# Query halves of every other tile for layer 1's product with the values

## The reference

```python
def _L1_attn_ref(x, w_attn, w_proj):
    B, T, N_EMBD, N_HEAD = (4, 1024, 96, 6)
    qkv = x @ w_attn
    q, k, v = jnp.split(qkv, 3, axis=-1)
    ...
    att = jnp.einsum('bqhd,bkhd->bhqk', q, k) * scale
    causal = jnp.tril(jnp.ones((t, t), dtype=bool))
    att = jnp.where(causal[None, None], att, jnp.finfo(att.dtype).min)
    att = jax.nn.softmax(att, axis=-1)
    out = jnp.einsum('bhqk,bkhd->bqhd', att, v).reshape(b, t, c)
    return out @ w_proj
```

## Time and profile before

| | |
|---|---|
| median of 3 runs | 2108.75 us (2106.65 to 2112.81) |
| span of the profiled execution | 2107.2 us |
| TensorE busy | 1847.2 us (88%) |
| VectorE busy | 1248.2 us (59%) |
| ScalarE busy | 1119.8 us (53%) |
| GpSimd busy | 144.7 us (7%) |

### The profile page before, as it was taken

One profiled execution on the slowest core, in us unless ns is written; L12 is line 12 of the kernel. 1 busy time (PEld: TensorE's weight loads), 2 busy tenths in 40 slices (PEclk: granted clock), 3 DMA queues, 4 the chain that ended last, 5 costly groups with the idle time before them and its releaser, 6 DMA issues.

```text
span 2107.2 us, 25342 instructions
## 1 busy us (share of the span) xinstructions
PE 1847.2 (88%) x9408; PEld 742.6 (35%) x9408; DVE 1248.2 (59%) x2508; ACT 1119.8 (53%) x1423; POOL 144.7 (7%) x69
## 2 busy tenths in 40 slices
PE   2697589998899988998899988999889988999858
PEld 1132233343234433343333432344333433334323
DVE  5671676546764667636765467636676466744631
ACT  2256345674456744675456744567345745555433
POOL 3000002000020000200020000200002000200000
PEclk7599599999999999999999999999999999999979
DMA  6416400354016320263003440163202630002100
GB/s 139 58 35 110 75 12 19 86 66 83 11 30 116 68 39 18 51 101 68 21 19 86 66 83 11 30 116 70 37 19 51 101 68 15 17 11 59 27 11 8
DMA packets 55699, 110.98 MB, mean 53 GB/s; under 512 B 17686, under 2 KB 18903, under 8 KB 54040
## 3 DMA queue, kind: packets, MB, share of 16 engines
q1 hardware_dynamic: 54040, 109.06, 27.5%
q10 hardware_dynamic: 1536, 0.30, 0.1%
HBM read 61.82 MB, written 34.60 MB: 46 GB/s over the span
## 4 chain that ended last, share of the span: by engine, by line
PE 68%; DVE 18%; ACT 5%; DMA 4%; issue 3%; SPq 1%; POOL 1%; ACTq 0%; DVEq 0%; POOLq 0%
PE psOM L645 16%; PE psS L591 12%; PE psT L620 8%; DVE mx L1279 8%; PE psT L621 7%; PE psT L755 6%; PE psS L769 4%; PE psT L623 4%; DVE mrow L1381 3%; PE psT L541 3%; DVE qb L1408 2%; DVE x L1390 1%; PE psT L550 1%; DMA qr<-negb 1%; PE psT L800 1%
## 5 line engine op out<-in xcount | busy, mean ns | idle before, releaser
L1006 ACT ACTIVATE probs<-psT 128x1024 f32<-128x1024 f32 (+7 forms) x768 | 622.7, 837 | 524.3 <-PE psT L621 258.2
L1279 DVE TENSOR_REDUCE mx<-psS 128x1 f32<-128x512 f32 (+3 forms) x1152 | 704.9, 643 | 286.2 <-PE psS L591 217.2
L621 PE MATMUL psT<-qb,kb 97*128 97x512 f32 x768 | 415.6, 585 | 0.0
L645 PE MATMUL psOM<-probs,v 128*32 128x512 f32 (+3 forms) x2688 | 383.3, 558 | 11.6 <-ACT probs L1006 11.6
L591 PE MATMUL psS<-ka,qa 128*128 128x512 bf16 x768 | 298.8, 400 | 38.9 <-DVE mx L1279 19.8
L620 PE MATMUL psT<-qa,ka 128*128 128x512 bf16 x768 | 296.8, 386 | 11.8 <-DVE resid L1268 5.1
L755 PE MATMUL psT<-xf,w1s 97*128 97x512 f32 x384 | 187.8, 623 | 2.1 <-DVE mrow L1381 1.8
L623 PE MATMUL psT<-qr,kr 97*128 97x512 bf16 (+3 forms) x576 | 184.2, 349 | 4.3 <-DMA qr<-negb 3.3
L1408 DVE TENSOR_TENSOR qb<-psOM,qa 32x768 fp32r<-32x768 f32 x128 | 121.8, 952 | 101.6 <-ACT qa L1046 99.7
L769 PE MATMUL psS<-probs,w2s 128*96 128x512 f32 x384 | 180.7, 596 | 0.8 <-ACT att L1071 0.8
L591 PEld LDWEIGHTS psS<-ka,qa 128*128 128x128 bf16 x768 | 71.5, 97 | 308.8 <-DVE mx L1279 244.3
(11 more groups left out here) (146 smaller groups left out, 1651.3 us busy)
## 6 DMA issues: line engine op xcount, KB each, us to landing
scr<-split SPq DMA_DIRECT2D x32, 576.0 KB, 4.4
scr<-qb SPq DMA_DIRECT2D x16, 768.0 KB, 6.8
qr<-scr SPq DMA_DIRECT2D x48, 192.0 KB, 6.5
au<-ot SPq DMA_DIRECT2D x192, 32.0 KB, 2.0
lb<-ot SPq DMA_DIRECT2D x192, 32.0 KB, 2.0
qr<-scr SPq DMA_DIRECT2D x48, 128.0 KB, 4.4
kr<-scr SPq DMA_DIRECT2D x48, 128.0 KB, 7.3
qa<-scr SPq DMA_DIRECT2D x32, 128.0 KB, 3.7
```

The lines of the kernel that those rows point to most:

```text
L621: last = mm(o[:, a:b], kb[:, h, ks], qb[:, h, a:b], start=False, stop=True)
L645: last = mm(psO[j:j + 2 * HD, a - c * HALF:HALF], v[:, kt, 2 * p + hh, :], probs[:, (2 * kt + hh) % 4, a:(c + 1) * HALF], start=kt == 0, s ...
L1006: A(probs[:, n % 4, q0:T], psT[:, t_slot(ts, m), q0:T], ACT.Exp).then_inc(t_free, 1)
L1279: V.reduce_max(mx[layer][:, p % 2, (h % 2) * NT + t, kc:kc + 1], psS[:, s_bank(st, fill), 0:max_cols(layer, t, kc)], AX).then_inc(s_free, 1)
```

## The change

In layer 1's value product, a query half c now is the query tiles c, c + 2, c + 4, c + 6, in place of the tiles 4 c to 4 c + 3. For key tile kt, half 0 has the even query tiles from kt on, and half 1 the odd ones. The tiles of a half stand side by side in psO as before, so the moving operand is read from probs as blocks of 128 columns that lie 256 apart. att then holds the tiles in that order, and `res_norm` finds tile t at column 128 x `tile_at(1, t)`. Layer 0's matmuls are those of before, in another branch of the code.

```diff
@@ -216,6 +216,11 @@
 def att_m(layer, p):
 
     return ("attn1", p - 1) if layer else ("attn0", p - 1) if p else ("lead", 0)
+
+
+def tile_at(layer, t):
+
+    return t % NC * (NT // NC) + t // NC if layer else t
 
 
 def next_layer0(it):
@@ -629,7 +634,6 @@
 
                 def values(p, kt):
 
-                    q0 = q_from(layer, kt)
                     if kt == 0:
                         if layer == 1 and p == 0:
                             pe.wait_ge(y_free, upto("y_free", it, st, 0))
@@ -638,12 +642,18 @@
                         ts, n = att_t(layer, (p * NT + kt) * 2 + hh)
                         pe.wait_ge(t_free, upto("t_free", it, ts, n + 1))
                         for c in range(NC):
-                            a, j = max(q0, c * HALF), 32 * (2 * hh + c)
-                            if a >= (c + 1) * HALF:
+                            j = 32 * (2 * hh + c)
+                            if layer == 0:
+                                last = mm(psO[j:j + 2 * HD, :], v[:, kt, 2 * p + hh, :],
+                                          probs[:, (2 * kt + hh) % 4, c * HALF:(c + 1) * HALF], start=kt == 0,
+                                          stop=kt == NT - 1)
                                 continue
-                            end = NT if layer == 0 else (c + 1) * HALF // P
-                            last = mm(psO[j:j + 2 * HD, a - c * HALF:HALF], v[:, kt, 2 * p + hh, :],
-                                      probs[:, (2 * kt + hh) % 4, a:(c + 1) * HALF], start=kt == 0, stop=kt == end - 1)
+                            first = (kt + NC - 1 - c) // NC
+                            if first == NT // NC:
+                                continue
+                            every = probs[:, (2 * kt + hh) % 4, :].rearrange("p (i c q) -> p c i q", c=NC, q=P)
+                            last = mm(psO[j:j + 2 * HD, first * P:HALF], v[:, kt, 2 * p + hh, :], every[:, c, first:],
+                                      start=kt == 0, stop=kt == NT - NC + c)
                         last.then_inc(p_used, 1)
 
                 n = PER_PAIR[layer]
@@ -705,8 +715,8 @@
                     pe.wait_ge(s_free, upto("s_free", it, "norm", b - 1))
                     for i in range(4):
                         t = 4 * b + i
-                        last = mm(psS[:, b, i * C:(i + 1) * C], att[0:C, t * P:(t + 1) * P], wp[1][:, :], start=True,
-                                  stop=True)
+                        a = tile_at(1, t) * P
+                        last = mm(psS[:, b, i * C:(i + 1) * C], att[0:C, a:a + P], wp[1][:, :], start=True, stop=True)
                     last.then_inc(s_full, 1)
 
             def tr_norm(it):
```

## The result

The change takes 2084.61 us (median of 4 runs, 2080.04 to 2088.35) where the kernel before takes 2110.78 (4 runs). The ratio is 0.9884, 95% interval 0.9868 to 0.9901. The profiled execution spans 2084.2 us, 23.0 less than before.

The account below looks back on a forecast made before the run. TensorE was taken as the bound (68% of the chain). Pairs gaining 0.88, 1.03 and 0.88 us give 2.8 an image, 22.5 in all with the last image's extra; 2107.2 - 22.5 = 2084.7, plus 1.5 gives 2086, range 2078 to 2102.

Parts of the forecast that it names:

- The block costs its longest half: Layer 1 value blocks: each costs its longest half, 0.21 us per 128 columns; the shorter half is free.
- More records are free: Value blocks kt 4, 5 and 6: four more matmul records each cost only about 0.01 us a block.
- A record for a pass: TensorE's float32 matmuls: each leaves two records, taken to be its two passes.
- the price of the slow reads: Rival, value products' reads with jumps: 1.3 ns a column more, 6 us a pair, 144 in all, about 2230; chance 0.03.
- kt 6 doesn't count: Layer 1 block kt 6: its 0.20 us cut only lengthens TensorE's following wait for ScalarE, so the pair gains nothing.
- kt 5 counts in the second pair alone, 0.05 elsewhere: Layer 1 block kt 5: 0.20 us gained in the second pair; 0.05 in first and third, where the transpose needs mrow.
- VectorE keeps out of the way: Layer 1 maxima: VectorE's idle gaps behind blocks stay positive, by 0.13 us at the tightest, so kt 2, 3, 4 count.
- The first rival: VectorE or ScalarE takes over in second and third pair; only the first gains, 7 us, time 2101.5; chance 0.10.
- The clock at nought: Granted clock over the whole run: dips may move the time some 5 us either way; put at 0.
- The second rival: A clock dip is added in the second or third pair: 1.8 us an image, 14 in all, 2100.5; chance 0.05.
- the sign that I had named for it: Third pair, counterpart of 1052 to 1074 us: a granted clock under 1.00 would show the forecast wrong.
- Reads with jumps: Layer 1 value products: reading runs of 128 columns with 128 left out between costs nothing, taken as zero.

## Why the prediction was right

2086 was forecast and 2084.6 measured; for the profiled spans 2084.7 and 2084.2. By steps:

**The block costs its longest half.** Right: 0.85, 0.85, 0.64, 0.64 and 0.43 us, the figures of the forecast. The split into runs of two tiles put kt 2 back to 1.07 and its pair up by 0.23.

**More records are free.** Right, 0.64 for eight records of 256 columns against 0.63 for four. The Trainium skill, page "TensorEngine Tiling (Array Packing)", section Instruction Overhead, gives each matmul some 60 cycles; by the prediction's estimate from that, 25 ns a record, such a block would have been at 0.73. The trace does not agree.

**A record for a pass.** The prediction takes the two records of a float32 matmul for its two passes. The traces show two records and no number of passes: 128 columns more cost 0.21 us over the two, where in bfloat16 they cost about 0.06 (after the change a matmul of 512 columns starts 0.22 us ahead of the next, at 788.78, and one of 384 starts 0.16 ahead, at 792.21). Nothing of the sum hangs on it; the price of the slow reads, 6 us a pair, does.

**kt 6 doesn't count.** Right, and tested: 0.44 us in kt 4, nothing in kt 6, for the same columns; 0.9 us in the one pair that has neither transpose nor next pair behind it.

**kt 5 counts in the second pair alone, 0.05 elsewhere.** Right in the first pair (0.88, as forecast) and the third (0.89), and VectorE's mrow is what the transpose waits for there: in the third pair it starts 0.05 us behind mrow's end, where it was 0.11, in the first 0.06 for 0.10. No run took kt 5 by itself.

```profile
1059.46 0.18 DVE L1294 TENSOR_TENSOR mrow<-mx 128x16 f32<-128x16 f32 x1
1059.69 0.28 PE L606 MATMUL psOM<-cst,mrow 128*16 128x128 f32 x1
```

**VectorE keeps out of the way.** Here a term was mis-sized. The second pair gained 0.90, not 1.03. I had set the cut of 0.41 us behind kt 4 against VectorE's gap of 0.54 and kept 0.13. But two maxima follow that block, and the second needs the bank that VectorE is still reducing: the pair of L596 at 794.93 takes 0.75 us where the two of L591 came through in 0.60 before (1048.32). VectorE's gap, of which the prediction kept 0.13, is gone there, and its reductions run on through the next block:

```profile
1048.32 0.60 PE L591 MATMUL psS<-ka,qa 128*128 128x512 bf16 x2
...
792.10 4.55 DVE L1289 TENSOR_REDUCE mx<-psS 128x1 f32<-128x512 f32 x7 [0.26 <-PE psS L596]
```

The first rival was thus true for 0.14 us of one pair, 1 us in all; the run with kt 4 longer gave back 0.30 there and 0.44 in the third pair. In the last image's third pair 0.90 came for 1.1.

**The clock at nought.** Right in the sum, by luck: two errors met. The second rival happened in five images, 3.4 us at half clock each, at a price of 1.06 us and not 1.8, and the first pairs lost 2.8 us more; the stretches outside the pairs gave 9.9. The forecast of the edit alone, 22.5 us, was 1.1 too high, and 1.6 came from the clock. I gave the second rival 0.05, and it came, in the second pair; the sign that I had named for it looked at the third pair alone, which stayed at 1.00. Its reason, that the low stretches come where TensorE is less loaded, is half of what the rows show: before the change TensorE was busy 2.50 of the 5.20 us ahead of the fall at 1004.2, but all of the 3.50 us ahead of the one at 1171.5.

**Reads with jumps.** Right: 207.1 us with and without.

## What to carry to other kernels

Here products that share the array by column groups cost their longest member, so a causal or ragged dimension should be dealt to the groups like cards and not cut in blocks; the work is the same, the longest share is not. Ask of each shortened piece what the next wait is anchored to: in front of a wait it gives nothing, and a gap of a neighbour engine has to hold every instruction of its ring that follows, not only the first. Where the time of the whole scatters by some microseconds, compare the lengths of one repeated stretch at full clock: here they repeat within 0.03 us in a profile, and told apart what medians 10 us off the expectation did not.

## What the runs showed of the hardware

The granted clock fell to half (1.2 of 2.4 GHz) for 3.4 us in five of eight second pairs, a stretch whose TensorE was busy 0.84 of the time before the change, after its blocks had got 0.2 to 0.4 us shorter; it fell right behind a wait of 1.36 us, and twelve full-array matmuls in that wait kept it up. Matmuls of one column group in a row can hold up the next group: with three of 128 columns in a row (kt 6 longer) the groups start some 0.25 us apart and the block takes 1.59 us, where 0.87 was expected from the columns; with two of 256 in a row (kt 4 longer) all four start within 0.04 us and it takes 1.09, as expected. And the DMA of 16 rows of negated maxima took 1.7 to 1.8 us from issue to landing in nearly all cases, but 2.0 to 3.1 in one to four of some profiles' 48, at no fixed place.
